# Step 0 of a one-core attention and tile-FFN kernel: x in two halves, first weights split on GpSimd, array warmed by 512-column products

## The chip, the cores and the metric

One core of a Trainium2 chip runs the whole program. The metric is device time in microseconds. Three runs of the kernel before gave 309.85, 310.03 and 310.3; their median is 310.03.

## The reference, cut to what matters

x has shape (2, 2048, 256). Two residual blocks follow one another:

```
h   = gelu(layernorm(x) @ W1{q,k,v} + b1{q,k,v});  q, k, v = h @ W2{q,k,v} + b2{q,k,v}
x  += layernorm(((q @ k.T) / sqrt(256*512) * tril) @ v) * ln_w + ln_b
idx = argmax_t(position_table(2048, 32) @ sign(tile_sigs).T)      # one tile of 8 for each position
x  += layernorm(x) @ W[idx].T + b[idx]
```

The choice of a tile depends on the position table and the signs of the tile signatures alone, not on x.

## The kernel before, in words

The 4096 rows are worked off in 8 steps of 512 rows (4 steps for each batch element). Every product with float32 inputs is made of three fp32r products: each operand is split into a rounded part ("hi") and its rest ("lo"), and hi*hi + hi*lo + lo*hi is accumulated. So every weight needs two operations before its first use: a copy that rounds it into `w_sp[:, i, 0]`, and a subtraction that writes the rest into `w_sp[:, i, 1]`. The weights are numbered 0 to 5: W1q, W1k, W1v, W2q, W2k, W2v. Weight 3 is scaled first, and weight 5 has its row means taken off first (`w_mean`, counted by the semaphore `w_even`).

A step's front part is: layer norm of x into `xn`; 8 transposes into two PSUM banks; rounding and rest of `xnT`; six groups of 6 products of 512 columns for the hidden layer (`front_h`), each followed by gelu and rounding on ScalarE (`hidden`) and the rest on VectorE (`h_rest`); then q, k, v, the transposes of k (`front_ktok`) and the scores. The back part (state and output of linear attention) of step s is interleaved with the front part of step s+1. There is no scheduler: each engine's program is written out by hand in the order in which it runs, and engines wait for each other's semaphores. An engine never goes past an instruction that waits.

Step 0 has extra work. TensorE runs `route_scores` between the first transposes and the first hidden group: 16 products of the position table (`peT`, laid over `hT`) with the signs `sgn_r`, which wait for the table's transfer (`table_in`) and for three small VectorE operations (`route_signs`, semaphore `rv`). GpSimd makes constants (identity, triangles, a blank row), the reciprocal standard deviations (`rstd_lead`, whose central operation is a power), and `residual(0)`, which adds the layer norm's bias row to x. VectorE runs `route_argmax` and `route_ranks` for the choice of tiles. The statistics of step 1's x (`lead_stat(1)`, `lead_var(1)`, `rstd_lead(1)`) are made during step 0 too, and ScalarE normalises x of step 1 (`lead_norm(1, ...)`) in four pieces between `q_rounded`, `k_rounded` and `v_rounded` of step 0.

## Time and profile before

| | |
|---|---|
| median of three runs | 310.03 us |
| span of the profiled execution | 307.9 us (2.1 us less than the median) |
| TensorE busy | 289.4 us, 94% of the span |
| VectorE, ScalarE, GpSimd busy | 75%, 64%, 53% |
| first hidden product of step 0 starts | 12.72 us |
| first transposes of step 1 start | 36.34 us |

A timeline row gives the start in us, the time it covers in us, the engine, the line of the kernel, the operation, the tiles written and read with their shapes, how many instructions were merged, and in brackets how long the engine had been idle and what ended that. Busy shares are averages; in step 0 the engines wait for each other far more than in the later steps.

### The profile page before, as it was taken

The numbers are of one execution on the slowest core, as the hardware profiler recorded it, in microseconds if no ns is written. First come the engines' busy times: TensorE is split into PE (matmuls) and PEld (weight loads), VectorE is DVE, ScalarE is ACT, GpSimd is POOL, SyncE is SP. The second block draws the span as 40 slices with busy tenths as digits, with TensorE's granted clock in tenths as the row PEclk, the third lists the DMA queues.
The fourth block names the chain that finished last, engine by engine and source line by source line (L and its number), as shares of the span: only waits on it lengthen the run. The fifth ranks groups of instructions, "written<-read, shape, count | busy, mean of one in ns | idle before, by whom it ended". The sixth has DMA issues, their size and how long they took to land.

```text
span 307.9 us, 5596 instructions
## 1 busy us (share of the span) xinstructions
PE 289.4 (94%) x1874; PEld 259.1 (84%) x1874; DVE 231.8 (75%) x514; ACT 198.4 (64%) x391; POOL 163.3 (53%) x229
## 2 busy tenths in 40 slices
PE   6899999999999999999999999999999898889990
PEld 6778989898789889888978898889898898889970
DVE  4697779789977966986697579758956888767661
ACT  2388567767586778578667865886877554688000
POOL 3710622190479174927544653557364575777771
PEclk9989999999999999999999999999999999999997
DMA  8819961001110211111131100027021361393220
GB/s 203 285 43 245 362 206 34 0 2 68 34 57 18 90 51 38 42 60 38 36 104 36 56 18 0 2 73 200 2 92 36 88 198 55 126 333 119 80 68 18
DMA packets 24193, 27.84 MB, mean 90 GB/s; under 512 B 4643, under 2 KB 22052, under 8 KB 24102
## 3 DMA queue, kind: packets, MB, share of 16 engines
q1 hardware_dynamic: 15750, 13.29, 14.6%
q0 software_dynamic: 3296, 8.64, 8.1%
q10 hardware_dynamic: 5120, 5.55, 5.6%
q8 instruction: 16, 0.26, 0.4%
q14 instruction: 11, 0.09, 0.1%
HBM read 13.95 MB, written 14.44 MB: 92 GB/s over the span
## 4 chain that ended last, share of the span: by engine, by line
PE 59%; DVE 18%; issue 5%; DMA 5%; ACT 5%; POOL 4%; SPq 1%; POOLq 0%; DVEq 0%; ACTq 0%
PE ring L463 33%; PE o_ps L463 9%; PE s_ps L463 5%; PE sc_ps L463 5%; POOL out_dram L1688 3%; DMA w_stage<-w1v 3%; DVE xres L1179 2%; PE ring L476 2%; PE w_ps L463 1%; PE ring L557 1%; DMA slot_rows<-sorted_rows 1%; DVE xnT L1098 1%; DMA sorted_rows<-xres,slot_i 1%; DVE st L1186 1%; DVE hT L1103 1%
## 5 line engine op out<-in xcount | busy, mean ns | idle before, releaser
L463 PE MATMUL ring<-xnT,w_sp 128*128 128x512 f32 x288 | 75.0, 406 | 2.1 <-issue 1.0
L463 PEld LDWEIGHTS ring<-xnT,w_sp 128*128 128x128 f32 x288 | 53.1, 193 | 14.8 <-DVE hT L1103 1.9
L836 ACT ACTIVATE ring<-ring,b_cols 128x512 f32<-128x512 f32 x48 | 31.7, 660 | 24.5 <-PE ring L463 23.4
L463 PE MATMUL ring<-hT,w_sp 128*128 128x512 f32 x192 | 46.4, 397 | 0.0
L1103 DVE TENSOR_TENSOR hT<-ring,hT 128x512 fp32r<-128x512 f32 x48 | 32.6, 684 | 13.9 <-ACT hT L839 13.3
L463 PEld LDWEIGHTS ring<-hT,w_sp 128*128 128x128 f32 x192 | 35.4, 188 | 8.1 <-DVE hT L1103 0.2
L1643 POOL DMA_INDIRECT sorted_rows<-xres,slot_i x30 | 30.7, 1023 | 8.4 <-issue 6.6
L1609 POOL TENSOR_TENSOR vtok<-v,vtok 128x512 fp32r<-128x512 f32 x14 | 17.7, 1282 | 30.7 <-ACT vtok L858 30.7
L1590 POOL TENSOR_SCALAR nm<-mv 128x4 f32<-128x4 f32 x8 | 1.8, 229 | 57.5 <-DVE mv L1085 57.5
L839 ACT CAST hT<-ring 128x512 fp32r<-128x512 f32 x48 | 28.2, 587 | 1.5
L463 PE MATMUL o_ps<-state,qT 128*128 128x256 f32 x174 | 26.6, 290 | 0.0
L1688 POOL DMA_INDIRECT out_dram<-slot_rows x22 | 21.6, 980 | 6.7 <-issue 6.1
L463 PE MATMUL s_ps<-vtok,ktok 128*128 128x256 f32 x168 | 24.9, 285 | 0.0
L463 PEld LDWEIGHTS o_ps<-state,qT 128*128 128x128 f32 x174 | 23.2, 190 | 1.4 <-issue 0.5
L463 PEld LDWEIGHTS ring<-w_sp,hT 128*128 128x128 f32 x192 | 23.4, 188 | 0.6
L463 PE MATMUL ring<-w_sp,hT 128*128 128x256 f32 x192 | 23.9, 281 | 0.0
L1179 DVE SCALAR_TENSOR_TENSOR xres<-cen,rs,xres 128x256 f32<-128x256 f32 x32 | 22.1, 703 | 0.3 <-issue 0.3
L463 PEld LDWEIGHTS s_ps<-vtok,ktok 128*128 128x128 f32 x168 | 22.1, 191 | 0.0
L463 PE MATMUL sc_ps<-qT,kT 128*128 128x128 f32 (+1 forms) x174 | 21.7, 281 | 0.0
L1109 DVE SCALAR_TENSOR_TENSOR qT<-ring,b_cols,qT 128x512 fp32r<-128x512 f32 x16 | 12.0, 751 | 12.3 <-ACT qT L845 12.3
L463 PEld LDWEIGHTS sc_ps<-qT,kT 128*128 128x128 f32 x174 | 20.4, 192 | 0.2
L1151 DVE TENSOR_TENSOR state<-s_ps,state 128x512 fp32r<-128x512 f32 x27 | 18.3, 677 | 2.4 <-ACT state L878 2.4
(210 smaller groups left out, 614.2 us busy)
## 6 DMA issues: line engine op xcount, KB each, us to landing
sorted_rows<-blank ACTq DMA_DIRECT2D x1, 5032.0 KB, 18.1
xt<-x SPq DMA_DIRECT2D x8, 512.0 KB, 3.5
slot_rows<-sorted_rows SPq DMA_DIRECT2D x22, 136.0 KB, 3.0
w_stage<-tile_w SPq DMA_DIRECT2D x8, 256.0 KB, 2.8
h<-sorted_rows SPq DMA_DIRECT2D x15, 136.0 KB, 3.6
hT<-position_table POOLq DMA_DIRECT2D x1, 512.0 KB, 6.5
sorted_rows<-xres,slot_i POOLq DMA_INDIRECT x30, 2.6
row_stage<-rows ACTq DMA_DIRECT2D x1, 384.0 KB, 7.7
```

The costliest lines, as they stand in the source:

```text
L463: last = te.matmul(o, lhs[k][a], rhs[k][c], start=start and k == 0 and i == 0, stop=stop and k == n - 1 and i == 2, skip_group_check=check)
L476: last = te.transpose(ring[k][:, cols(c)], xn[:, c, cols(k)], ident[:, :])
L557: last = te.transpose(ring[(14 + n) % 3][:, cols(i)], k32[:, i % 2, cols(2 * n + i // 2)], ident[:, :])
L836: nc.scalar.activation(full, ring[(2 + m) % 3][:, :], ACT.Gelu, bias=b1c[:, m // 2, m % 2:m % 2 + 1]).then_inc(gelu, 1)
L839: nc.scalar.copy(hT[:, m, 0, :], full).then_inc(h_hi, 1)
L1103: nc.vector.tensor_tensor(hT[:, m, 1, :], ring[(2 + m) % 3][:, :], hT[:, m, 0, :].bitcast(F32), ALU.subtract).then_inc(h_lo_dve, 1)
L1109: nc.vector.scalar_tensor_tensor(out=qT[:, 1, j, :], in0=ring[(8 + j) % 3][:, :], scalar=b2c[:, Q, j:j + 1], in1=qT[:, 0, j, :].bitcast(F3 ...
L1151: nc.vector.tensor_tensor(state[:, 1, :], s_ps[:, :], state[:, 0, :].bitcast(F32), ALU.subtract).then_inc(s_lo, 1)
L1179: nc.vector.scalar_tensor_tensor(out=xres[s % XR][:, c, 0:C], in0=cen[:, c, :], scalar=rs2[:, c:c + 1], in1=xres[s % XR][:, c, 0:C], op0=A ...
L1609: nc.gpsimd.tensor_tensor(vtok[:, 1, 2 * j:2 * j + 2, :], v32[:, 2 * j:2 * j + 2, :], vtok[:, 0, 2 * j:2 * j + 2, :].bitcast(F32), ALU.sub ...
L1643: pool.indirect_dma_start(out=sorted_rows, out_offset=bass.IndirectOffsetOnAxis(ap=at, axis=0), in_=xres[s % XR][:, c, :], in_offset=None) ...
L1688: pool.indirect_dma_start(out=out_rows, out_offset=bass.IndirectOffsetOnAxis(ap=row_buf(n)[:, PLACE:PLACE + 1].bitcast(I32), axis=0), in_= ...
```

## The change

The change touches step 0 only. Half of x (two of four chunks) is loaded, normalised and transposed ahead of the other half. ScalarE rounds only weight 0 and VectorE makes only its rest; GpSimd does both for weights 1 to 5. GpSimd issues the position table's transfer after its constants and after the first half of x is there, where it was its first instruction. The rows `rows3` are loaded by the sync queue behind the weights, where ScalarE's queue loaded them, and x of step 1 comes last. `residual(0)` and `rstd_lead(1)` stand behind the five splits on GpSimd. On TensorE, 34 transposes of the identity are replaced by 8 products of 512 columns ahead of the first transposes and 4 more between the two halves of them.

```diff
-WARM = 34
+WARM = (8, 4)
@@ sync
-            load_x(0)
+            sp.dma_start(xt[0][:, 0:2, :], x_gbp[0, 0][:, 0:2]).then_inc(x_half, 16)
+            sp.dma_start(xt[0][:, 2:CH, :], x_gbp[0, 0][:, 2:CH]).then_inc(x_in[0], 16)
             for i, w in enumerate((w1[Q], w1[K], w1[V], w2[Q], w2[K], w2[V])):
                 sp.dma_start(w_stage[:, i, :, :], w.rearrange("(k p) n -> p k n", p=P)).then_inc(w_in[i], 16)
-                if i == 2:
-                    load_x(1)
+            sp.dma_start(row_stage[:, :, :], rows3.partition_broadcast(P)).then_inc(rows_in_place, 16)
+            load_x(1)
@@ tensor
+            def kept_busy(n):
+                for i in range(n):
+                    te.matmul(ring[2][:, :], warm_r[:, 0:P], warm_r[:, :], start=True, stop=True)
+
+            def first_transposes():
+                te.wait_ge(xn_half, 1)
+                for k in range(KC):
+                    for c in range(2):
+                        te.transpose(ring[k][:, cols(c)], xn[:, c, cols(k)], ident[:, :])
+                kept_busy(WARM[1])
+                te.wait_ge(xn_done, 1)
+                for k in range(KC):
+                    for c in range(2, CH):
+                        last = te.transpose(ring[k][:, cols(c)], xn[:, c, cols(k)], ident[:, :])
+                    last.then_inc(fill, 1)
...
+            te.wait_ge(warm_set, 1)
+            kept_busy(WARM[0])
             te.wait_ge(consts, 2)
-            for i in range(WARM):
-                te.transpose(ring[2][:, 0:P], ident[:, :], ident[:, :])
-            front_transposes(0, True)
+            first_transposes()
             route_scores()
@@ scalar
-            for i in range(5):
-                weights_rounded(i)
-                if i == 2:
-                    xnT_rounded(0)
-            act.wait_ge(small_in, 32)
+            act.wait_ge(w_in[0], 16)
+            nc.scalar.copy(w_sp[:, 0, 0, :, :], w_stage[:, 0, :, :]).then_inc(w1q_hi, 1)
+            xnT_rounded(0)
+            act.wait_ge(cols_in, 16)
             act.wait_ge(rp, 1)
             for m in range(6):
                 hidden(0, m)
-                if m == 2:
-                    weights_rounded(5)
@@ vector
+            nc.vector.memset(warm_r[:, :].bitcast(F32), 1.0).then_inc(warm_set, 1)
             state_cleared()
-            lead_stat(0)
-            lead_var(0)
+            first_half(0)
+            first_half(1)
+            first_norm(0)
+            first_norm(1)
+            dve.wait_ge(w1q_hi, 1)
+            nc.vector.tensor_tensor(w_sp[:, 0, 1, :, :], w_stage[:, 0, :, :], w_sp[:, 0, 0, :, :].bitcast(F32),
+                                    ALU.subtract).then_inc(w1q_lo, 1)
             route_signs()
-            weights_rest((0,))
-            lead_norm()
-
             xnT_rest(0)
-            weights_rest((1, 2))
@@ gpsimd
-            pool.dma_start(peT, pe).then_inc(table_in, 16)
             nc.gpsimd.memset(ident[:, :], 0.0).then_inc(consts, 1)
...
-            rstd_lead(0)
...
-            residual(0)
             nc.gpsimd.memset(blank[:, :], 0.0).then_inc(blank_set, 1)
             pool.wait_ge(blank_set, 1)
             nc.gpsimd.memset(blank[:, PLACE:PLACE + 1].bitcast(I32), NOWHERE).then_inc(blank_set, 1)
+
+            pool.wait_ge(x_half, 16)
+            pool.dma_start(peT, pe).then_inc(table_in, 16)
+            for h in range(2):
+                these = slice(2 * h, 2 * h + 2)
+                pool.wait_ge(var_first, h + 1)
+                nc.gpsimd.tensor_tensor(rs1[:, these], ve1[:, these], half[:, these], ALU.pow).then_inc(rstd_first, 1)
+
+            for i in range(1, 6):
+                pool.wait_ge(w_in[i], 16)
+                if i == 3:
+                    pool.wait_ge(w_scaled, 1)
+                elif i == 5:
+                    pool.wait_ge(w_even, 3)
+                nc.gpsimd.tensor_copy(w_sp[:, i, 0, :, :], w_stage[:, i, :, :]).then_inc(w_hi, 1)
+                pool.wait_ge(w_hi, i)
+                nc.gpsimd.tensor_tensor(w_sp[:, i, 1, :, :], w_stage[:, i, :, :], w_sp[:, i, 0, :, :].bitcast(F32),
+                                        ALU.subtract).then_inc(w_lo, 1)
+
+            pool.wait_ge(rows_in_place, 16)
+            residual(0)
             rstd_lead(1)
             v_rest(0)
```

Two new VectorE functions make one half each: `first_half(h)` runs two bn_stats, two bn_aggr and the addition of EPS, and `first_norm(h)` the two normalisations behind GpSimd's power. VectorE's `w_mean` work for weight 5 is spread between `h_rest(0, 0)`, `h_rest(0, 1)` and `h_rest(0, 2)`; `lead_stat(1)` stands behind `h_rest(0, 3)` and `lead_var(1)` behind `h_rest(0, 4)`.

On GpSimd, at the start of the program, the order before was this (`rs`, `nm`, `sh`, `ve` are the small tiles of `rstd_lead`; `hT<-position_table` is the table's transfer):

```order
L1573 DMA hT<-position_table 64x2048
L1574 MEMSET ident 128x128
...
L1593 TENSOR_TENSOR rs<-ve,half 128x4 [waits var1]
L1595 TENSOR_TENSOR sh<-nm,rs 128x4 [waits rstd1]
L1648 AFFINE_SELECT tril<-tril 128x128
...
L1602 TENSOR_TENSOR xres<-xt,row_stage 128x4x256
L1665 MEMSET blank 128x272
L1667 MEMSET blank 128x1 [waits blank_set]
L1590 TENSOR_SCALAR nm<-mv 128x4 [waits aggr1]
```

In the changed program the same place, from the last constants on, reads:

```order
L1686 MEMSET blank 128x272
L1688 MEMSET blank 128x1 [waits blank_set]
L1691 DMA hT<-position_table 64x2048 [waits x_half]
L1695 TENSOR_TENSOR rs<-ve,half 128x2 [waits var_first] x2
L1703 CAST w_sp<-w_stage 128x512 [waits w_in1]
L1705 TENSOR_TENSOR w_sp<-w_stage,w_sp 128x512 [waits w_hi]
...
L1703 CAST w_sp<-w_stage 128x512 [waits w_even,w_in5]
L1705 TENSOR_TENSOR w_sp<-w_stage,w_sp 128x512 [waits w_hi]
L1626 IOTA xres 128x4 [waits x_half,x_in0,rows_in_place]
L1627 TENSOR_TENSOR xres<-xt,row_stage 128x4x256
L1613 TENSOR_SCALAR nm<-mv 128x4 [waits aggr1]
```

The table's transfer moved from the first place to behind all constants, and ten split operations moved in ahead of `residual(0)` and of step 1's reciprocal deviations.

On VectorE, the changed program from the second half's normalisation to the mean of weight 5 reads (`w_sp<-w_stage,w_sp` is the rest of weight 0, `sgn` the signs for the routing):

```order
L1107 TENSOR_SCALAR xn<-xt,mv,rs 128x256 [waits rstd_first]
L1107 TENSOR_SCALAR xn<-xt,mv,rs 128x256
L1357 TENSOR_TENSOR w_sp<-w_stage,w_sp 128x512 [waits w1q_hi]
L1257 TENSOR_SCALAR sgn<-sig_in 64x8 [waits sigs_in]
L1258 TENSOR_SCALAR sgn<-sig_in 64x8 [waits rv]
L1259 TENSOR_TENSOR sgn_r<-sgn 64x8 [waits rv]
...
L1133 TENSOR_TENSOR hT<-ring,hT 128x512 [waits h_hi]
L1370 TENSOR_SCALAR w_mean<-w_mean 128x2 [waits w_even]
L1372 TENSOR_TENSOR w_stage<-w_stage,w_mean 128x512 [waits w_even]
L1133 TENSOR_TENSOR hT<-ring,hT 128x512 [waits h_hi]
```

The signs came ahead of the normalisation and now come behind it; weight 5's mean is taken off behind the second `h_rest`, where it was taken off ahead of the first.

## Rows read from the trace of the kernel before

**Rows 1.** The page, parts 1 and 2: busy time, and granted clock in tenths.

```profile
PE 289.4 (94%) x1874; PEld 259.1 (84%) x1874; DVE 231.8 (75%) x514; ACT 198.4 (64%) x391; POOL 163.3 (53%) x229
PEclk9989999999999999999999999999999999999997
```

**Rows 2.** Chain that ended last, 0 to 60 us: start, us, engine, tile, line.

```profile
30.92 0.39 DVE kT L1115
...
33.88 0.51 ACT vtok L858
```

**Rows 3.** Timeline of PE, 0 to 45 us.

```profile
9.82 1.09 PE L476 MATMUL ring<-ident,xn 128*128 128x128 f32 x8 [0.88 <-DVE xn L1091]
10.84 1.95 PE L608 MATMUL sc_ps<-sgn_r,hT 64*128 64x8 f32 x16
12.72 6.00 PE L463 MATMUL ring<-xnT,w_sp 128*128 128x512 f32 x18
...
36.34 1.06 PE L476 MATMUL ring<-ident,xn 128*128 128x128 f32 x8 [0.17 <-DVE ktok L1122]
```

**Rows 4.** Window 14 to 18 us: busy by engine, granted clock, DMA.

```profile
14.00:18.00 4.00, 4.00 (x12) 3.14 (x11) 3.19 (x7) 3.18 (x6) 0.00 (x0) 0.57 0.38 131
```

**Rows 5.** Timeline of POOL, 0 to 45 us.

```profile
1.33 0.72 POOL L1573 DMA_DIRECT2D hT<-position_table  x1 [0.83 <-POOLq L1763]
2.05 0.23 POOL L1574 MEMSET ident<- 128x128 f32 x1
...
3.06 0.20 POOL L1583 MEMSET tril<- 128x128 f32 x1
...
8.58 0.37 POOL L1648 TENSOR_SCALAR_AFFINE_SELECT tril<-tril 128x128 f32<-128x128 f32 x1
...
10.62 0.14 POOL L1662 IOTA row_no<- 128x1 f32 x1
...
10.81 2.35 POOL L1602 TENSOR_TENSOR xres<-xt,row_stage 128x1024 f32<-128x1024 f32 x1
13.11 0.32 POOL L1665 MEMSET blank<- 128x272 f32 x1
...
21.40 0.23 POOL L1590 TENSOR_SCALAR nm<-mv 128x4 f32<-128x4 f32 x1 [7.82 <-DVE mv L1085]
...
23.00 0.30 POOL L1595 TENSOR_TENSOR sh<-nm,rs 128x4 f32<-128x4 f32 x1
```

**Rows 6.** DMA issues by line: KB each, us to landing.

```profile
xt<-x SPq DMA_DIRECT2D x8, 512.0 KB, 3.5
...
hT<-position_table POOLq DMA_DIRECT2D x1, 512.0 KB, 6.5
```

**Rows 7.** Groups by line and shape, POOL: busy, mean ns.

```profile
L1609 POOL TENSOR_TENSOR vtok<-v,vtok 128x512 fp32r<-128x512 f32 x14 | 17.7, 1282 | 30.7 <-ACT vtok L858 30.7
...
L1677 POOL TENSOR_SCALAR w_stage<-w_stage 128x255 f32<-128x255 f32 x16 | 15.4, 966 | 0.0
...
L1623 POOL TENSOR_TENSOR rs<-ve,half 128x2 f32<-128x2 f32 x2 | 1.4, 708 | 0.2
```

**Rows 8.** Timeline of ACT, 0 to 45 us.

```profile
25.70 0.59 ACT L895 ACTIVATE xn<-xt,sh,rs 128x256 f32<-128x256 f32 x1
```

**Rows 9.** The page, part 5: the hidden layer's groups on ACT and DVE.

```profile
L836 ACT ACTIVATE ring<-ring,b_cols 128x512 f32<-128x512 f32 x48 | 31.7, 660 | 24.5 <-PE ring L463 23.4
...
L1103 DVE TENSOR_TENSOR hT<-ring,hT 128x512 fp32r<-128x512 f32 x48 | 32.6, 684 | 13.9 <-ACT hT L839 13.3
...
L839 ACT CAST hT<-ring 128x512 fp32r<-128x512 f32 x48 | 28.2, 587 | 1.5
```

**Rows 10.** Timeline of DVE, 0 to 45 us.

```profile
4.36 1.40 DVE L1077 BATCH_NORM_STATS2 st<-xt 128x6 f32<-128x256 f32 x4 [2.89 <-DMA xt<-x]
...
8.39 1.38 DVE L1091 TENSOR_SCALAR xn<-xt,mv,rs 128x256 f32<-128x256 f32 x4 [0.94 <-POOL rs L1593]
```

**Rows 11.** Line L1323 alone: duration ns min/median/max.

```profile
L1323 DVE TENSOR_TENSOR w_sp<-w_stage,w_sp x6: 679/686/1184, 6.8 to 22.6; 128x512 fp32r<-128x512 f32 x6
```

More of the change, by code:

```diff
@@ L100, in mk_seq_kernel @@
         ident = sb("ident", [P, P])
+        warm_r = sb("warm_r", [P, GT], F32R)
         tril = sb("tril", [P, P])
@@ L153, in mk_seq_kernel @@
         w_in = [sem(f"w_in{i}") for i in range(6)]
-        small_in = sem("small_in")
+        x_half = sem("x_half")
+        cols_in = sem("cols_in")
+        rows_in_place = sem("rows_in_place")
         sigs_in = sem("sigs_in")
@@ L166, in mk_seq_kernel @@
         w_lo = sem("w_lo")
+        w1q_hi = sem("w1q_hi")
+        w1q_lo = sem("w1q_lo")
+        warm_set = sem("warm_set")
         stat1 = sem("stat1")
         aggr1 = sem("aggr1")
+        aggr_first = sem("aggr_first")
+        var_first = sem("var_first")
+        rstd_first = sem("rstd_first")
+        xn_half = sem("xn_half")
         var1 = sem("var1")
@@ L499, in front_h @@
                         bank_free(s, m - 3)
-                    if first and m % 2 == 0:
-                        te.wait_ge(w_lo, m // 2 + 1)
+                    if first and m == 0:
+                        te.wait_ge(w1q_lo, 1)
+                    elif first and m % 2 == 0:
+                        te.wait_ge(w_lo, m // 2)
                     for k in range(KC):
@@ L515, in front_qk @@
                 if first:
-                    te.wait_ge(w_lo, 4 + which)
+                    te.wait_ge(w_lo, 3 + which)
                 for j in (2 * which, 2 * which + 1):
@@ L821, in _ @@
             act.dma_start(sig_in[:, :], sigs2).then_inc(sigs_in, 16)
-            act.dma_start(b_cols[:, :, :].rearrange("p a k -> p (a k)"), bias_cols).then_inc(small_in, 16)
-            act.dma_start(row_stage[:, :, :], rows3.partition_broadcast(P)).then_inc(small_in, 16)
+            act.dma_start(b_cols[:, :, :].rearrange("p a k -> p (a k)"), bias_cols).then_inc(cols_in, 16)
             act.wait_ge(consts, 3)
@@ L1073, in _, with first_half, first_norm @@
         def _(dve):
+            def first_half(h):
+                dve.wait_ge(x_in[0] if h else x_half, 16)
+                for c in (2 * h, 2 * h + 1):
+                    nc.vector.bn_stats(st1[:, c, :], xt[0][:, c, :]).then_inc(stat1, 1)
+                dve.wait_ge(stat1, 2 * h + 2)
+                alone(dve, gate_dve)
+                for c in (2 * h, 2 * h + 1):
+                    last = nc.vector.bn_aggr(mv1[:, c, :], st1[:, c, :])
+                last.then_inc(aggr_first, 1)
+                dve.wait_ge(aggr_first, h + 1)
+                these = slice(2 * h, 2 * h + 2)
+                nc.vector.tensor_scalar(ve1[:, these], mv1[:, these, 1], EPS, None, ALU.add).then_inc(var_first, 1)
+            def first_norm(h):
+                dve.wait_ge(rstd_first, h + 1)
+                for c in (2 * h, 2 * h + 1):
+                    last = nc.vector.tensor_scalar(xn[:, c, :], xt[0][:, c, :], mv1[:, c, 0:1], rs1[:, c:c + 1],
+                                                   ALU.subtract, ALU.mult)
+                last.then_inc(xn_done if h else xn_half, 1)
             def lead_stat(s):
@@ L1081, in lead_var @@
                 alone(dve, gate_dve)
-                if s:
-                    dve.wait_ge(shift1, s)
+                if s > 1:
+                    dve.wait_ge(shift1, s - 1)
                 for c in range(CH):
@@ L1086, in lead_var @@
                 last.then_inc(aggr1, 1)
-            def lead_norm():
-                dve.wait_ge(rstd1, 1)
-                for c in range(CH):
-                    last = nc.vector.tensor_scalar(xn[:, c, :], xt[0][:, c, :], mv1[:, c, 0:1], rs1[:, c:c + 1],
-                                                   ALU.subtract, ALU.mult)
-                last.then_inc(xn_done, 1)
             def xnT_rest(s):
@@ L1338, in _ @@
                                     ALU.mult).then_inc(w_scaled, 1)
-            weights_rest((3, 4))
+            h_rest(0, 0)
             dve.wait_ge(w_in[5], 16)
             nc.vector.tensor_reduce(w_mean[:, :], w_stage[:, 5, :, :], AX_X, ALU.add).then_inc(w_even, 1)
+            h_rest(0, 1)
             dve.wait_ge(w_even, 1)
@@ L1348, in _ @@
                                     w_mean[:, :].unsqueeze(2).broadcast_to([P, KC, C]), ALU.add).then_inc(w_even, 1)
-            dve.wait_ge(small_in, 32)
+            h_rest(0, 2)
+            dve.wait_ge(cols_in, 16)
             nc.vector.tensor_scalar(b2c[:, Q, :], b2c[:, Q, :], INV_SCALE, None, ALU.mult).then_inc(w_scaled, 1)
-            h_rest(0, 0)
-            h_rest(0, 1)
+            h_rest(0, 3)
             lead_stat(1)
+            h_rest(0, 4)
             lead_var(1)
-            h_rest(0, 2)
-            h_rest(0, 3)
-            weights_rest((5,))
-            h_rest(0, 4)
             h_rest(0, 5)
@@ L1361, in _ @@
             q_rest(0, (0,))
+            dve.wait_ge(w_lo, 3)
+            dve.wait_ge(rows_in_place, 16)
             route_argmax()
@@ L1667, in _ @@
             nc.gpsimd.memset(blank[:, PLACE:PLACE + 1].bitcast(I32), NOWHERE).then_inc(blank_set, 1)
+            pool.wait_ge(x_half, 16)
+            pool.dma_start(peT, pe).then_inc(table_in, 16)
+            for h in range(2):
+                these = slice(2 * h, 2 * h + 2)
+                pool.wait_ge(var_first, h + 1)
[12 more added lines that the diff above has]
+            residual(0)
             rstd_lead(1)
```

36 lines of the change are left out of this document (11 added, 25 removed).

## The prediction, made before the changed kernel was run

> **What bounds the kernel now.** I read the page first. TensorE is busy 94% of the span and holds its full clock in nearly every slice [rows 1]. So a microsecond gained or lost ahead of the steady part arrives at the end one for one, provided it shifts the first transposes of step 1, which start at 36.34 [rows 3]. That instant, T, is what I forecast.
>
> Then I read the timeline of TensorE for the first 37 us. The first hidden product stands at 12.72, straight behind the 16 routing products, which end then [rows 3]: with no idle time in between, TensorE itself, by its routing products, sets this start. The 18 products from 12.72 take 6.00 us [rows 3]. The granted clock falls to half there: the mean over 14 to 18 us is 0.57 [rows 4], which is 0.43 x 4 / 0.5 = 3.4 us at half clock (1.2 instead of 2.4 GHz), so 1.7 us of work lost. Ahead of the fall the array had had 0.88 us of idle, 8 transposes and 16 routing products of 8 columns [rows 3]. Without it a hidden product costs (6.00 - 1.7) / 18 = 0.24 us.
>
> From 25.7 to 36.3 the chain no longer lies on TensorE. It runs through the second rest of k (30.92), v, ScalarE's roundings of v (33.88) and the rest of ktok, which ends TensorE's wait ahead of T [rows 2, 3]. All of that stands behind ScalarE's queue, in which the first piece of step 1's normalisation starts at 25.70 [rows 8]. This normalisation needs GpSimd's `rstd_lead(1)`, which before was done at 23.3 [rows 5], with 2.4 us to spare.
>
> **The change part by part.**
>
> *Start of the hidden products.* x in halves, and five ScalarE and five VectorE operations fewer, bring `xn` and `xnT` forward. VectorE, with 1.40 us for four statistics and 1.38 for four normalisations [rows 10], has the second half done at about 8.2 (behind GpSimd's second power, below) instead of 8.39 + 1.38 = 9.77. But TensorE goes through the routing products first, and they wait for the table. Its transfer was GpSimd's first instruction and took 6.5 us from issue to landing [rows 6]. Now it stands behind the constants: 2.05 to 3.26 is 1.21 us, 8.58 to 10.76 is 2.18, and the blank row 0.32 plus 0.15 for its wait and last memset is 0.47 [rows 5]. Begun at about 1.0 (the first transfer's slot falls free), they end at 4.9. The first half of x is there by then, since the whole of it was used at 4.36 before [rows 10]. The table then lands at 4.9 + 6.5 = 11.4. The routing products occupy 10.84 to 12.72, 1.88 us [rows 3], so the hidden products start at 13.3, 0.6 us later than before. Bounds for the transfer: I don't expect it quicker than an x load of the same 512 KB, 3.5 us [rows 6], and 0.7 more for GpSimd's issue [rows 5], which gives 9.1; it is slower if it shares the engines with the later weights, by some 1 us. I take the transfer's own row, and 11.4, since both times other loads are under way.
>
> *The clock.* The 8 products come early (from about 1.5) and end by 5; the second lot of 4 stands between the transposes, at about 8 to 9.7. From then to the table's landing the array idles or runs narrow work, as it did before the fall in [rows 3, 4]. So I leave the 1.7 us of half clock where it was. The 34 transposes taken out were under no one's wait. If four products run at half clock, they cost 4 x 512 / 1.2 GHz = 1.7 us ahead of the last four transposes, and the table at 11.4 still hides that; without that cover they would cost 1 us.
>
> *The weights of the hidden layer.* GpSimd starts to split at about 7.4 (issue 0.72 [rows 5], then two powers at 0.71 [rows 7] and their waits). A split is a copy and a subtraction. The subtraction has the shape and types of `vtok<-v,vtok`, 1.28 us [rows 7]. The copy has no row. Below, it can't take less than the blank memset of 272 columns, 0.32 us [rows 5], brought to 512 columns, 0.6. Above, the tensor_scalar with 255 columns at 0.966 us [rows 7], brought to 512 columns, 1.9. A plain copy is nearer to the memset: I take 0.8, a split of 2.2 us with its wait. Splits of weights 1 to 4 end at 16.2, and the hidden and q products that want them start at 13.3 + 12 x 0.24 + 1.7 = 17.9 and later (weight 1 is split at 9.6). So these splits are hidden, up to the copy's upper end too (four of 3.3 us end at 20.6, weight 4 is wanted at 25).
>
> The page "GPSIMD Engine Reference", section 3.1, of the Trainium skill gives 1.03 cycles for an element of a one-input body; by that the copy would take about 0.6 us and the sum below would be 0.2 us smaller. No row here shows such a copy.
>
> *Weight 5 and what stands behind it.* This is the part that costs. GpSimd waits for `w_even` = 3, which VectorE gives only behind `h_rest(0, 1)`. From the start of the hidden products: 12 products at 0.24 with the half clock, 2.9 + 1.7 = 4.6; gelu and rounding 0.66 + 0.59 with waits 1.4; the rest 0.68 [rows 9]; subtracting the mean, of the same size, with its scaling and waits 1.0. Sum 7.7: 13.3 + 7.7 = 21.0. Then on GpSimd: split 2.2, to 23.2; `residual(0)` 2.35 plus 0.15 for its iota and wait [rows 5], to 25.7; `rstd_lead(1)` from 21.40 to 23.30, 1.9 [rows 5], to 27.6. The other input, `lead_var(1)`, is ready before 25.7: behind 24 products (5.7 + 1.7), 1.4 for ScalarE, 0.7 for `h_rest(0, 3)`, 1.4 of statistics, 0.7 for `h_rest(0, 4)` and 0.5 it is 13.3 + 12.1 = 25.4.
>
> *What then waits.* ScalarE's first normalisation of step 1 can't start before 27.6; before, it ran at 25.70 [rows 8]. Queued behind it are q's second rounding, the second piece, and k's four operations. Back to back these end with k's first rounding 3.1 us behind 27.6, VectorE takes the first rest and the three small operations on the bias row, 1.56 us, and starts the second rest of k at 27.6 + 4.66 = 32.3 instead of 30.92 [rows 2]: 1.4 us later. Everything from there to T was tight (v, its roundings and ktok follow one another in the chain [rows 2]), so T moves to 37.7.
>
> *Rest.* `residual(0)` comes 12 us later, so x of step 2 is loaded at about 25.7 beside the blank rows; it is wanted near 45, and the tile weights at 36, so I count nothing; without that cover it would be the time by which a load of some 5 us is late. Moving `rows3` behind the weights costs nothing: its first user is VectorE at 26. Sum: 310.03 + 1.4 = **311.4 us** (the profiled execution: 307.9 + 1.4 = 309.3).
>
> **The rivals.**
>
> *Faster: the table isn't late, and the clock holds.* If the transfer lands by about 10, the routing starts when the signs and transposes are done, the hidden products at about 12.0, and with the 12 wide products just ahead the array may escape the half clock. Then `w_even` = 3 comes at 12.0 + 6.0 = 18.0, `rstd_lead(1)` ends at 24.6, the second rest of k starts at 29.3, 1.6 us earlier: 308.4. It decides from 26.3 on: that is the end of `rstd_lead(1)` at which T stays. For it: wide products are real work, and the transfer's own minimum is lower than 6.5 us. Against: the same narrow routing work stands ahead of the hidden products as before. Chance 0.23.
>
> *The change does little.* Table early but half clock kept, or late with the clock kept: `rstd_lead(1)` at 26.3, plus or minus 0.6, so 309.5 to 310.6. Chance 0.2.
>
> *Signs late, by the port.* VectorE's one rest of a weight that met GpSimd's long addition took 1184 ns where the median is 686 [rows 11]: it started at 12.53, inside 10.81 to 13.16 [rows 5]. Now the rest of weight 0 and the signs (from about 8.2) fall among GpSimd's splits, of 0.8 and 1.28 us in turn. If each of the four waits out one of them, the signs are ready at 12.7, the hidden products start at 14.6, and the time is 312.8. Against: the signs are tiny and two have one input. Chance 0.12.
>
> The page "SBUF — State Buffer", section "SBUF: two separate sides", of the Trainium skill says that VectorE and GpSimd share a port pair under an exclusive lock, taken by VectorE operations with two SBUF inputs or in a two-port mode. By that rule the 1184 ns agree.
>
> The forecast itself, table about 11.4 and weight 5's split ahead of `rstd_lead(1)`, has 0.45.
>
> **How the numbers follow.** A measurement of this kernel tells 0.2%, 0.6 us. Slower by more than that: 0.45 + 0.12 = 0.57; within: 0.2; faster: 0.23. Low end: the faster rival at 308.4. High end: the copy at 1.9 instead of 0.8 adds 1.1 to the forecast, 312.5, and the port rival gives 312.8; both with a table 0.3 later, 313.1. Range 308.4 to 313.1; that of the likeliest case alone is 310.7 to 312.5.
>
> **What would show it.** Right: TensorE idle ahead of its routing products, ended by the table's transfer, near 11.4; the first hidden product near 13.3; a fall of the granted clock in the hidden products; GpSimd idle ahead of the last copy until `w_mean`; ScalarE idle ahead of `xn<-xt,sh,rs` until GpSimd's `sh`, near 27.6; T near 37.7. Wrong: a table that lands before 10, hidden products all at 0.24 us, no wait of ScalarE for `sh`, or a wait for weights 1 to 4 on TensorE (GpSimd's copy far above 1.9 us, or transfers late).

## The result, and the profile after

The changed kernel takes 315.42 us (median of 4 runs, 314.28 to 315.79). The kernel before took 309.94 beside it (309.77 to 310.3). The ratio is 1.0165, with a 95% interval of 1.0148 to 1.0182: 5.5 us slower, where 1.4 had been forecast. The ratios of this document leave out executions more than 1.5% above the fastest of the same kernel (2 of 12 in f2, 3 in f3, 3 in g1, 2 in g3), so that a ratio can differ a little from that of the medians, which count all. The profiled execution of after took 314.28, the lowest of the four. Its span is 312.4 us against 307.9, so 4.5 us of the loss stand in the trace.

TensorE is busy a little more than before, in a longer span, and stays the bound (the page, part 1, of after).

```profile
PE 290.8 (93%) x1852; PEld 259.0 (83%) x1852; DVE 232.2 (74%) x512; ACT 195.5 (63%) x386; POOL 172.3 (55%) x237
```

The next rows are the timeline of PE of after (start, time covered, engine, line, operation, tiles, count, idle time before it and what ended that). They answer to [rows 3].

```profile
7.12 1.08 PE L489 MATMUL ring<-ident,xn 128*128 128x128 f32 x4 [1.82 <-DVE xn L1107]
7.85 2.06 PE L483 MATMUL ring<-warm_r 128*128 128x512 f32 x4
9.71 1.05 PE L494 MATMUL ring<-ident,xn 128*128 128x128 f32 x4
13.57 3.54 PE L636 MATMUL sc_ps<-sgn_r,hT 64*128 64x8 f32 x16 [2.81 <-DMA hT<-position_table]
17.04 10.00 PE L474 MATMUL ring<-xnT,w_sp 128*128 128x512 f32 x36
...
40.59 1.06 PE L502 MATMUL ring<-ident,xn 128*128 128x128 f32 x8 [0.27 <-DVE ktok L1152]
```

T, the first transposes of step 1, is 40.59 instead of 36.34: 4.25 of the 4.5 us are lost ahead of it. The first hidden product moved from 12.72 to 17.04, which is 4.3 us by itself. Two rows make it. The array stands idle for 2.81 us until the table's transfer ends, and the 16 routing products then take 3.54 us, where they took 1.95 [rows 3]. Behind them the 36 hidden products take 9.84 us (17.04 to 26.88), 0.9 us less than before (12.72 to 23.45), and from there to T it is 13.71 us instead of 12.89, 0.8 us more: 4.3 - 0.9 + 0.8 is the 4.25 by which T moved.

The chain that ended last of after, 0 to 50 us (start, us, piece), runs through the same places:

```profile
4.29 9.14 DMA hT<-position_table
...
13.57 3.54 PE sc_ps L636 x16
17.11 4.32 PE ring L474 x12
...
23.57 0.70 DVE w_stage L1372
24.40 0.61 POOL w_sp L1703
25.09 1.29 POOL w_sp L1705
26.47 2.38 POOL xres L1627
...
30.44 0.21 POOL sh L1618
30.68 0.60 ACT xn L922
...
35.18 0.16 DVE kT L1145
```

Twelve hidden products at full clock would be 2.9 us; 4.32 says that part of them ran at half clock (1.2 instead of 2.4 GHz) too. Behind them stand weight 5's mean (L1372), its split, the residual and step 1's reciprocal deviations. ScalarE waits for the last of these, as the timeline of ACT of after shows:

```profile
30.68 0.60 ACT L922 ACTIVATE xn<-xt,sh,rs 128x256 f32<-128x256 f32 x1 [1.45 <-POOL sh L1618]
```

The timeline of POOL of after, against [rows 5] and [rows 7]:

```profile
4.02 0.10 POOL L1688 MEMSET blank<- 128x1 int32 x1
4.29 0.74 POOL L1691 DMA_DIRECT2D hT<-position_table  x1 [0.16 <-issue]
...
7.16 0.61 POOL L1703 CAST w_sp<-w_stage 128x512 fp32r<-128x512 f32 x1
7.85 1.28 POOL L1705 TENSOR_TENSOR w_sp<-w_stage,w_sp 128x512 fp32r<-128x512 f32 x1
...
26.43 2.42 POOL L1627 TENSOR_TENSOR xres<-xt,row_stage 128x1024 f32<-128x1024 f32 x1
```

The constants end at 4.12, not 4.9, so the transfer was issued 0.6 us earlier than forecast; the copy takes 0.61 us, not 0.8. The transfer is what was mis-sized. These are the parts 3 of the page for two stretches of after, from its issue to 8.2 us and from there to its landing (packets, MB, share of the 16 engines):

```profile
q1 hardware_dynamic: 1262, 1.21, 99.6%
q0 software_dynamic: 1, 0.01, 0.8%
...
q1 hardware_dynamic: 501, 0.73, 66.7%
q0 software_dynamic: 79, 0.52, 42.5%
```

And the same of the kernel before, from 4.2 us, before which q0 has no packet, to its landing:

```profile
q0 software_dynamic: 80, 0.52, 63.9%
q1 hardware_dynamic: 267, 0.26, 28.5%
q10 hardware_dynamic: 206, 0.20, 21.4%
```

q0 is the queue on which GpSimd's transfers go, the table's 80 packets here. Before, they began 2.9 us after the issue, behind 672 packets of SP's queue (q1, 1.3 to 4.2 us), and moved in 3.6 us, beside 473 packets of the weights and of q10, half of the engines' time. After, they began 3.9 us after it, behind 1262 packets that kept the engines full, and took 5.3 us beside 501, two thirds of the engines' time. That is 9.1 instead of 6.5. That the packets ahead and beside make the difference fits these rows; no run isolates it.

VectorE's timeline of after shows its operations beside GpSimd's splits, which run from 7.16 to 11.41:

```profile
6.24 0.73 DVE L1107 TENSOR_SCALAR xn<-xt,mv,rs 128x256 f32<-128x256 f32 x2
7.23 2.04 DVE L1107 TENSOR_SCALAR xn<-xt,mv,rs 128x256 f32<-128x256 f32 x2 [0.27 <-POOL rs L1695]
9.20 1.09 DVE L1357 TENSOR_TENSOR w_sp<-w_stage,w_sp 128x512 fp32r<-128x512 f32 x1
10.21 1.22 DVE L1257 TENSOR_SCALAR sgn<-sig_in 64x8 f32<-64x8 f32 x1
11.47 0.16 DVE L1258 TENSOR_SCALAR sgn<-sig_in 64x8 f32<-64x8 f32 x1
```

The same two normalisations take 0.73 us alone and 2.04 beside the first split. A row of 8 elements takes 1.22 and ends with the split, and the next two, behind it, take 0.16 each. The signs are ready at 11.83, and the table hides it.

### The profile page after: what moved, and what is told of

Same layout as the page of the kernel before. It is cut to its first block, busy times and chain, and to the rows that moved or that the text cites. A ratio compares the mean times of both kernels' runs of the same rounds, so it can differ in the third digit from the quotient of the medians.

```text
span 312.4 us, 5556 instructions
## 1 busy us (share of the span) xinstructions
PE 290.8 (93%) x1852; PEld 259.0 (83%) x1852; DVE 232.2 (74%) x512; ACT 195.5 (63%) x386; POOL 172.3 (55%) x237
## 3 DMA queue, kind: packets, MB, share of 16 engines
q0 software_dynamic: 3296, 8.64, 8.0%
## 4 chain that ended last, share of the span: by engine, by line
PE 61%; DVE 15%; POOL 7%; ACT 6%; DMA 5%; issue 4%; POOLq 0%; SPq 0%; DVEq 0%; ACTq 0%
PE ring L474 33%; PE o_ps L474 9%; PE s_ps L474 5%; PE sc_ps L474 5%; POOL out_dram L1730 3%; DMA hT<-position_table 3%; PE w_ps L474 2%; PE ring L502 2%; DVE xres L1209 2%; PE ring L585 1%; DMA slot_rows<-sorted_rows 1%; PE sc_ps L636 1%; DVE st L1216 1%; DVE hT L1133 1%; PE w_ps L628 1%
## 5 line engine op out<-in xcount | busy, mean ns | idle before, releaser
L474 PEld LDWEIGHTS s_ps<-vtok,ktok 128*128 128x128 f32 x168 | 22.1, 191 | 0.0
L1730 POOL DMA_INDIRECT out_dram<-h x15 | 15.7, 1044 | 8.2 <-issue 4.1
```

The lines of the kernel that those rows point to most:

```text
L474: last = te.matmul(o, lhs[k][a], rhs[k][c], start=start and k == 0 and i == 0, stop=stop and k == n - 1 and i == 2, skip_group_check=check)
L1730: pool.indirect_dma_start(out=out_rows, out_offset=bass.IndirectOffsetOnAxis(ap=row_buf(n)[:, PLACE:PLACE + 1].bitcast(I32), axis=0), in_= ...
```

## The experiments

Each kernel was timed beside the kernel before on its chip, and the ratio is what counts. On the three chips of the experiments the kernel before takes 322.5 to 323.4 us, not 309.9. The changed kernel, repeated there (f1 below), has T at 41.01, near its 40.59, but a span of 323.9 instead of 312.4. So some 11 us lie behind T, and nearly all of them behind the transposes of step 7, the last step (217.75 in f1, 217.20 in after): from there to the end f1 takes 106.2 us and after 95.2. Its row of granted clocks on the page is lower in the last slices than [rows 1], which is a part of it (40 slices of 8 us):

```profile
PEclk9569999999999999999999999999999999998698
```

All kernels of the experiments show it, and why it is so stays open. The kernel before was not traced there; g4 below, which measured the same as it (1.0012), has T at 36.62, so 36.34 serves as a measure within some 0.3 us.

**First round: one part each.** e1, from the changed kernel, issues the table's transfer first again:

```diff
+            pool.dma_start(peT, pe).then_inc(table_in, 16)
             nc.gpsimd.memset(ident[:, :], 0.0).then_inc(consts, 1)
...
-            pool.wait_ge(x_half, 16)
-            pool.dma_start(peT, pe).then_inc(table_in, 16)
```

> The changed kernel with the position table's transfer back as GpSimd's first instruction. Theory A (the late table holds up the routing products, and with them all hidden products): the table lands near 8, the routing products start when the signs are ready near 11.8, the first hidden product moves from 17.04 to between 13.8 and 15.4, and the time falls by 1.6 to 3.3 us, to 312.1 to 313.8. Rival B (GpSimd's chain of splits, residual and reciprocal deviations sets the first transposes of step 1 whatever the table does): under 0.5 us less than the changed kernel's 315.4.

Measured: 326.87 against 322.71, ratio 1.0116 [1.0074, 1.0158]. The table landed at 9.6, and yet little came back: Theory A wanted 1.6 to 3.3 us, and the interval overlaps that of the changed kernel on the experiments' chips (f1, 1.0121 to 1.0178), so that no gain is shown. PE's timeline of e1:

```profile
13.20 2.96 PE L636 MATMUL sc_ps<-sgn_r,hT 64*128 64x8 f32 x16 [2.54 <-DVE sgn_r L1259]
```

and DVE's:

```profile
10.62 0.69 DVE L1357 TENSOR_TENSOR w_sp<-w_stage,w_sp 128x512 fp32r<-128x512 f32 x1 [2.71 <-ACT w_sp L933]
11.23 0.57 DVE L1257 TENSOR_SCALAR sgn<-sig_in 64x8 f32<-64x8 f32 x1
...
12.03 1.11 DVE L1259 TENSOR_TENSOR sgn_r<-sgn 64x8 fp32r<-64x8 f32 x1
```

A second wait stood behind the first. With the table issued early, weight 0 landed 8.2 us after its issue instead of 4.3 (6.7 and 6.0 in f2 and g1, whose table is early too, but 4.0 in the kernel before), and its rest is ahead of the signs in VectorE's order; then the signs, beside GpSimd's split from 10.76 on, took 0.57 and 1.11 us instead of 0.16. They were ready at 13.1. The array, after 2.5 us of idle time, fell to half clock again: the granted clock is 0.97 from 12 to 14 us and 0.50 from 14 to 20.

e2, from the changed kernel, warms with the old 34 transposes and without the 4 wide products:

```diff
-                kept_busy(WARM[1])
...
-            te.wait_ge(warm_set, 1)
-            kept_busy(WARM[0])
             te.wait_ge(consts, 2)
+            for i in range(34):
+                te.transpose(ring[2][:, 0:P], ident[:, :], ident[:, :])
```

> The changed kernel with the 34 transposes of the identity in place of the 8 and 4 wide products. Theory A: the wide products end too early and leave the array idle, so the clock is at half through the routing products (3.5 us instead of 1.95) and into the hidden ones; with the transposes, which run until about 7, the clock may be up for the routing products: 0.5 to 2 us less than 315.4. Rival B: the array idles for 4 us behind the transposes of xn either way, the clock is down either way, and the time stays within 0.5 us of 315.4.

Measured: 327.15, ratio 1.0141 [1.0117, 1.0165]. PE's timeline has the same picture, as Rival B said, so the wide products neither make the loss nor prevent it:

```profile
13.42 3.54 PE L635 MATMUL sc_ps<-sgn_r,hT 64*128 64x8 f32 x16 [3.60 <-DMA hT<-position_table]
```

e3 makes only the table late in the kernel before:

```diff
-            pool.dma_start(peT, pe).then_inc(table_in, 16)
             nc.gpsimd.memset(ident[:, :], 0.0).then_inc(consts, 1)
...
+            pool.wait_ge(x_in[0], 16)
+            pool.dma_start(peT, pe).then_inc(table_in, 16)
             exact = dict(allow_small_or_imprecise_dtypes=True)
```

> The kernel before with one edit: the table's transfer is issued near 4.4 us, behind the first x, instead of at 1.33. Theory A: it lands near 13.4, the first hidden product starts at 15.4 to 17, and the time is 312.7 to 314.3, most of what the whole change costs. Rival B (the rest of the change is what costs): the transfer lands by 11 as its 6.5 us say, and the time is 310.0 to 310.8.

Measured: 329.06, ratio 1.0204 [1.0178, 1.0230]: this one edit costs 2.0%, no less than the whole change and more than Theory A's 2.7 to 4.3 us. Issued at 5.04, the table landed at 17.0, 3.6 us later than in after. So e3 shows that a late table alone can cost this much, but not how much of the change's own loss it makes. The page of e3 gives the transfer (KB, us to landing), longer still than in after:

```profile
hT<-position_table POOLq DMA_DIRECT2D x1, 512.0 KB, 12.0
```

and PE's timeline the wait and the half clock behind it:

```profile
17.22 3.54 PE L608 MATMUL sc_ps<-sgn_r,hT 64*128 64x8 f32 x16 [6.24 <-DMA hT<-position_table]
```

e4 gives the kernel before only GpSimd's splits of weights 1 to 5, with `residual(0)` and `rstd_lead(1)` behind them:

```diff
-            for i in range(5):
-                weights_rounded(i)
-                if i == 2:
-                    xnT_rounded(0)
+            act.wait_ge(w_in[0], 16)
+            nc.scalar.copy(w_sp[:, 0, 0, :, :], w_stage[:, 0, :, :]).then_inc(w1q_hi, 1)
+            xnT_rounded(0)
...
+            for i in range(1, 6):
...
+                nc.gpsimd.tensor_copy(w_sp[:, i, 0, :, :], w_stage[:, i, :, :]).then_inc(w_hi, 1)
...
+            residual(0)
             rstd_lead(1)
```

> The kernel before with one edit: GpSimd splits weights 1 to 5, with residual(0) behind them, nothing else moved. Theory A (the splits themselves are cheap, 1.95 us each, and ready in time when the mean of weight 5 is taken off early): GpSimd ends rstd_lead(1) near 25.5, ScalarE isn't held up, and the time is 309.3 to 310.4. Rival B (GpSimd is too slow for five splits): ScalarE waits for sh by 1 us and more, 311 or more.

Measured: 321.57 (12 runs), ratio 0.9976 [0.9960, 0.9992]: a small gain, and the only one of the study. The profiled execution is the fastest of the twelve (320.40), and g2 below, which keeps the splits, doesn't repeat the gain. ScalarE waited 0.59 us for `sh`, against the expectation. PE's timeline of e4 has the first 18 hidden products without half clock, then a new wait:

```profile
12.70 4.47 PE L465 MATMUL ring<-xnT,w_sp 128*128 128x512 f32 x18
18.12 4.68 PE L465 MATMUL ring<-xnT,w_sp 128*128 128x512 f32 x18 [0.95 <-DVE hT L1104]
```

VectorE comes late with the rests because its small operations take longer beside the splits, as one row of its timeline shows (on `b_cols`, 0.25 us in the trace of after at 24.78):

```profile
16.23 1.25 DVE L1351 TENSOR_SCALAR b_cols<-b_cols 128x2 f32<-128x2 f32 x1
```

**Second round: the changed kernel again, and three repairs of it.** f1 is the changed kernel, unedited, for the chip's own ratio.

> The changed kernel itself, unaltered, as the measure for the three that follow on the same chip. Expected: 1.4 to 1.8% slower than the kernel before, the table's transfer landing near 13.4, the routing products near 3.5 us long.

Measured: 326.85 against 322.49, ratio 1.0150 [1.0121, 1.0178]; the table took 8.7 us, the routing products 3.54 from 13.10. The window 14 to 18 us of f1 (busy and count of PE, PEld, DVE, ACT, POOL, then granted clock, DMA) shows half clock outright:

```profile
14.00:18.00 4.00, 4.00 (x16) 3.71 (x16) 0.00 (x0) 0.00 (x0) 3.33 (x4) 0.50 0.03 10
```

f2 has e1's edit, and the signs ahead of the normalisation:

```diff
             first_half(1)
+            route_signs()
             first_norm(0)
...
-            route_signs()
             xnT_rest(0)
```

> The changed kernel with the table's transfer as GpSimd's first instruction, and the signs made ahead of first_norm. With the table alone moved, the signs came at 13.2, behind weight 0's rest, and took the table's place as what is waited for. Theory A (two things hold up the routing products, table and signs, one behind the other): they now start behind the transposes of xn, at 10.5 to 11, the first hidden product at 12.7 to 14.4, and the time is 2 to 4 us less than the changed kernel's. Rival B (weights that land later, since the table goes ahead of them, set the start: weight 0 lands near 10, its rest is ready near 11.5): less than 1.5 us.

Measured: 322.75 (12 runs), ratio 0.9990 [0.9960, 1.0021], as Theory A said. No loss is left that the interval would show. PE's timeline of f2 has no idle time ahead of the routing, which runs at full clock, and T is 36.55. Among the 36 hidden products the clock still falls (0.57 from 14 to 18 us):

```profile
11.04 1.95 PE L636 MATMUL sc_ps<-sgn_r,hT 64*128 64x8 f32 x16
12.91 10.23 PE L474 MATMUL ring<-xnT,w_sp 128*128 128x512 f32 x36
```

f3 leaves the late table and puts 7 wide products into the gap:

```diff
             first_transposes()
+            kept_busy(7)
             route_scores()
```

> The changed kernel with 7 more wide products between the transposes of xn and the routing products, where the array idled for 2.8 us. Theory A (the idle array runs the routing products at half clock, 3.5 us instead of 1.95): routing products of 1.95 to 2.6 us, and 1 to 2 us less than the changed kernel. Rival B (the routing products are slow whatever stands ahead of them, or the half clock is only put off to the hidden products): within 0.6 us of the changed kernel.

Measured: 323.88 (12 runs), ratio 1.0024 [0.9990, 1.0059]. PE's timeline of f3: the table is no earlier than 12.4, but the routing products and the 36 hidden ones behind them run at full clock (0.24 each). T is 36.59, 4.4 us earlier than in f1: 0.6 because the table landed that much earlier in this execution (8.1 us instead of 8.7), 1.6 by the routing products, and 2.2 by the hidden ones (8.53 us to the end of the 36, where f1 takes 10.74). Theory A counted only the routing products. The rows:

```profile
10.22 1.86 PE L483 MATMUL ring<-warm_r 128*128 128x512 f32 x7
12.50 1.92 PE L636 MATMUL sc_ps<-sgn_r,hT 64*128 64x8 f32 x16 [0.42 <-DMA hT<-position_table]
14.35 8.69 PE L474 MATMUL ring<-xnT,w_sp 128*128 128x512 f32 x36
```

f4 leaves both and takes weight 5 off the chain. Its mean and step 1's statistics come ahead of `h_rest(0, 0)`, and `rstd_lead(1)` ahead of the residual:

```diff
-            h_rest(0, 0)
+            lead_stat(1)
...
-            h_rest(0, 1)
+            lead_var(1)
...
+            h_rest(0, 0)
+            h_rest(0, 1)
             h_rest(0, 2)
...
+            rstd_lead(1)
             pool.wait_ge(rows_in_place, 16)
             residual(0)
-            rstd_lead(1)
```

> The changed kernel with lead_stat(1), the mean of weight 5 and lead_var(1) ahead of h_rest(0, 0), where VectorE idled for 7.9 us, and with rstd_lead(1) ahead of residual(0) on GpSimd. Theory A (the chain that was forecast, weight 5, residual, reciprocal deviations, costs by itself what ScalarE waits for sh, and part of that was hidden by TensorE): ScalarE's wait of 1.45 us ahead of xn is gone, the first transposes of step 1 come 0.7 to 1.1 us earlier, and so does the end. Rival B (that chain is hidden entirely by the late hidden products): no change beyond 0.3 us.

Measured: 325.58, ratio 1.0097 [1.0068, 1.0126], 1.3 us less than f1 by the medians, with intervals that overlap by little. ACT's timeline of f4 has no wait for `sh`, which POOL had ready at 22.1:

```profile
27.64 0.59 ACT L922 ACTIVATE xn<-xt,sh,rs 128x256 f32<-128x256 f32 x1
```

In its profiled execution the routing products took 2.04 us behind a wait of 1.99 us for the table, so that its T (38.29) owes 1.5 us to the clock. What the freed chain gives is read behind the hidden products: from the end of the 36 to T it is 12.97 us here and 13.70 in f1, 0.7 us less, the low end of what was expected.

**Third round: can it be beaten?** g1 is f2 and f4 together, with the scaling of `b_cols` moved up to the signs.

> The changed kernel with all repairs: table first, signs (and the scaling of the q bias) ahead of first_norm, lead_stat(1), the mean of weight 5 and lead_var(1) ahead of h_rest(0, 0), rstd_lead(1) ahead of residual(0). Theory A (these waits add up): 1 to 1.5 us less than with table and signs first alone, which measured the same as the kernel before: ratio to the kernel before 0.994 to 0.998, first transposes of step 1 near 35.3. Rival B (freeing the chain only moves VectorE operations into GpSimd's splits, which they then wait out): ratio 0.998 to 1.002.

Measured: 324.76 against 323.44 (12 and 35 runs), ratio 1.0020 [0.9983, 1.0058]: no better than f2, and outside what Theory A expected. From the end of the 36 hidden products to T it is 12.89 us, as in the kernel before, so the chain is free here too. But with no idle time ahead of them the routing products took as long as at half clock, and T is 38.68:

```profile
11.40 3.57 PE L636 MATMUL sc_ps<-sgn_r,hT 64*128 64x8 f32 x16
```

g2 is e4 with the mean of weight 5 behind one `h_rest`, `b_cols` ahead, `lead_var(1)` one `h_rest` later, and `rstd_lead(1)` ahead of the residual.

> The kernel before with GpSimd's splits (0.9976 of the kernel before), and now also the first h_rest between the mean's operations, the q bias scaled ahead of them, and rstd_lead(1) ahead of residual(0). Theory A: TensorE's wait of 0.95 us ahead of the fourth hidden group and ScalarE's of 0.59 go, first transposes near 34.6, ratio 0.993 to 0.997. Rival B: VectorE's small operations wait out GpSimd's splits wherever they stand, ratio stays at 0.9976.

Measured: 323.99, ratio 1.0030 [0.9998, 1.0062]. The idle time of e4 fell from 0.95 to 0.32 + 0.23 us, and T is 35.32, 0.2 us earlier than e4's (34.6 was expected). The time didn't follow, and in this trace 2.0 us were lost in step 1. GpSimd's `residual(1)` came 4 us later than in e4, behind a wait of 4.94 us for the tile's bias, and stood beside an operation of VectorE of 32 elements, which takes 0.21 us in e4 and before (rows of POOL and DVE of g2):

```profile
44.35 2.39 POOL L1603 TENSOR_TENSOR xres<-xt,row_stage 128x1024 f32<-128x1024 f32 x1
44.35 2.43 DVE L1252 TENSOR_TENSOR held<-w_stage 128x32 f32<-128x32 f32 x1
```

The transposes of step 2 start 30.82 us behind T, in e4 28.81.

g3 is g1 with 3 wide products ahead of the routing (`kept_busy(3)`).

> The kernel with all repairs and 3 wide products between the transposes of xn and the routing products. Theory A (wide products just ahead of the narrow ones keep the clock up into the hidden products): they delay the hidden products by 0.3 to 0.7 us but save the 1.7 us of the half-clock stretch in some executions: 0.3 to 1 us less than without. Rival B: the clock falls anyway, 0.3 to 0.7 us more than without.

Measured: 325.84, ratio 1.0059 [1.0022, 1.0095]. That is 0.4% above g1, with intervals that overlap, so the three products gave nothing. In its profiled execution x came late (TensorE waits 6.96 us ahead of its first transposes, in the other changed kernels 1.8 to 2.5), so no row of it is read.

g4 is the kernel before with 14 wide products in place of the 34 transposes.

```diff
-            for i in range(WARM):
-                te.transpose(ring[2][:, 0:P], ident[:, :], ident[:, :])
+            te.wait_ge(warm_set, 1)
+            for i in range(14):
+                te.matmul(ring[2][:, :], warm_r[:, 0:P], warm_r[:, :], start=True, stop=True)
```

> The kernel before with 14 products of 512 columns in place of the 34 transposes, nothing else. Theory A (what is run to warm the array doesn't matter while the narrow routing products stand behind it): ratio 0.998 to 1.002, clock down for some 3.4 us in the hidden products as before. Rival B (the wide products hold the clock): 1 to 1.7 us less, ratio 0.995 to 0.997.

Measured: 324.12, ratio 1.0012 [0.9977, 1.0048], with a first lot of 18 hidden products of 5.99 us from 12.92 and a granted clock of 0.57 from 14 to 18, as in [rows 3, 4]. Wide products in the place of transposes change nothing that can be measured here.

**All traces side by side.** One execution of each kernel, in us: idle time of TensorE ahead of the routing products, the time these take, from the first of the 36 hidden products to the end of the last, from there to T, T, and the start of the transposes of step 7.

| | idle ahead | routing | 36 hidden | from there to T | T | step 7 |
|---|---|---|---|---|---|---|
| before | 0 | 1.95 | 10.73 | 12.89 | 36.34 | 212.73 |
| after | 2.81 | 3.54 | 9.84 | 13.71 | 40.59 | 217.20 |
| f1, after again | 2.65 | 3.54 | 10.74 | 13.70 | 41.01 | 217.75 |
| e1, table first | 2.54 | 2.96 | 10.61 | 13.72 | 40.42 | 217.16 |
| e2, old warming | 3.60 | 3.54 | 10.93 | 13.71 | 41.53 | 218.05 |
| e3, before, table late | 6.24 | 3.54 | 10.79 | 12.89 | 44.37 | 220.92 |
| e4, before, splits | 0 | 1.95 | 9.94 | 12.88 | 35.52 | 211.87 |
| f2, table and signs first | 0 | 1.95 | 10.07 | 13.57 | 36.55 | 213.28 |
| f3, gap filled | 0.42 | 1.92 | 8.53 | 13.71 | 36.59 | 213.33 |
| f4, chain freed | 1.99 | 2.04 | 10.68 | 12.97 | 38.29 | 214.65 |
| g1, all repairs | 0 | 3.57 | 10.89 | 12.89 | 38.68 | 215.06 |
| g2, e4 reordered | 0 | 1.94 | 9.60 | 12.88 | 35.32 | 213.92 |
| g4, before, wide | 0 | 1.95 | 10.80 | 12.90 | 36.62 | 213.00 |

Three things can be read off. From the hidden products' end to T it is 13.57 to 13.72 us wherever weight 5's split and the residual stand ahead of `rstd_lead(1)` in the changed kernel, and 12.88 to 12.97 everywhere else: that chain costs 0.6 to 0.8 us. The routing products took 2.96 to 3.54 us in the five traces with 2.5 us and more of idle time ahead of them, and 1.92 to 2.04 in the others, g1 excepted, which had none and took 3.57. And behind the transposes of step 7 the kernels of the experiments take from 106.2 to 109.6 us, in no order that their edits in step 0 would explain. So one total can carry 3 us that have nothing to do with step 0, and T and step 7 tell more of an edit than a single time.

## Why the prediction was right and wrong

The direction was right, and so was the path that was forecast; the size was off by 4.0 us, outside the range. Of these, 2.9 are in T (40.59 instead of 37.7), 0.2 behind it in the trace, and 0.9 lie between trace and median (after's median is 3.0 us above its span, before's 2.1). By its steps:

*Start of the hidden products* is the term that failed. Forecast: table at 11.4, hidden products at 13.3. Measured: 13.43 and 17.04. Of the 3.7 us between, 2.0 are the transfer and 1.7 the routing products. The transfer was given its old 6.5 us "since both times other loads are under way", and took 9.1 (8.7 in f1, 12.0 in e3). The load is not alike in the two places: before, 672 packets of SP's queue went ahead of it, now 1262. The price named for that in the prediction, "some 1 us", was too low by 1.6, and it wasn't taken into the sum; the earlier issue (4.29 instead of 4.9) gave 0.6 back. That the table alone can carry the loss is shown by e3 (2.0%); that an early table and early signs remove it, by f2 (0.999).

*The clock* is the second part of the same failure. I left the 1.7 us of half clock where it was. In after, the routing products take 3.54 instead of 1.95, 1.6 us more, and the 36 hidden ones 9.84 (17.04 to 26.88) where 36 x 0.24 is 8.64, 1.2 us more: 2.8 in all, of which 1.6 stand ahead of the first hidden product, where none had been put. The prediction saw the idle time ahead of the routing but gave it no price beyond that of before, where it was 0.88 us ahead of the transposes. How much the clock is worth, f3 shows: with the gap filled and the table still late the kernel is at 1.0024, and of the 4.4 us between its T and f1's the clock makes 3.8. What decides the clock in one execution is not settled: f4's routing, behind 1.99 us of idle time, was at full clock, and g1's, behind none, was not.

*The weights of the hidden layer.* Right: splits 1 to 4 ended at 17.5 (16.2 forecast), and TensorE waited for none. GpSimd waited 2.21 us for the scaling of weight 3, which the sum left out and which cost nothing. The copy took 0.61, not 0.8. The prediction's estimate from the Trainium skill ("GPSIMD Engine Reference", section 3.1), 0.6 us, agrees with the row; the page's 1.03 cycles for an element alone give an estimate of 512 x 1.03 / 1.2 GHz = 0.44 us, to which a fixed part has to be added.

*Weight 5 and what stands behind it.* Right in itself. From the first hidden product to the mean took 7.2 us (17.04 to 24.26; forecast 7.7), from there to `sh` 6.4 (to 30.64; forecast 6.6). The end, 30.64 instead of 27.6, carries the 3.7 us from above less the 0.7 by which these two terms were too long; that they offset a part of the miss is luck.

*What then waits.* Right: ScalarE waited 1.45 us for `sh`, and from its normalisation to the second rest of k it was 4.5 us (30.68 to 35.18; forecast 4.7). What this chain costs by itself is 0.7 us ahead of T in the traces (f4 against f1) and 1.3 us by their medians, which the clock moves too; that this is near the 1.4 forecast for the whole is chance, since the forecast had the chain and the later start together.

*Rest.* Right: from T to the end it is 271.8 us in after and 271.6 before.

*The rivals.* What the port rival expected did happen, though it wasn't the cause in after: the second half's normalisation was done at 9.27, not at 8.2, and the stretched signs at 11.83, behind the table's cover. With the cover gone (e1) they cost most of what the early table should have given, together with the late weight 0, which the prediction hadn't foreseen. The Trainium skill's page "SBUF — State Buffer", section "SBUF: two separate sides", reserves the lock to VectorE operations with two SBUF inputs or in a two-port mode. The measured one-input normalisations waited too (2.04 against 0.73). One-input rows are quicker than two-input ones in after (the scaling of 128x512 in L1363 takes 0.42 us, a subtraction of that size 0.69), which would fit such a mode; that they ran in it no run shows. The faster rival needed the table by 10. f2 had it, at 8.0 by issue plus transfer (1.33 + 6.7), and ended level, not 1.6 us faster: the half clock stayed, 1.4 us of it among the hidden products, and ScalarE still waited 1.31 us for `sh`.

*Where the change's own gain went.* With both waits removed (f2), half the x, ten splits on GpSimd and the wide products are worth 0.1% with an interval that holds zero. The splits alone gave 0.24% in e4, with an interval that ends at 0.9992; T and step 7 agree in size (0.8 and 0.9 us earlier than before). In g2 their gain is at T and is lost again in step 1.

What stays open: why the transfer on GpSimd's queue starts 3 to 4 us after its issue and takes 6.0 to 12.0 us; why weight 0 lands late behind an early table in the changed kernel and not before; what chooses the clock in one execution. Early signs with a late table were not run; by the trace of after they would have nothing to give, being ready 1.6 us ahead of the table as it is. The 1.1 us by which the median of after lies beyond its profiled execution (315.42 - 314.28) are not explained by one trace.

## What to carry to other kernels

A transfer's duration is no fixed property of it: the same 512 KB took 6.0 to 12.0 us here. When its issue is moved behind other loads, count the packets of every queue that are then ahead of it and beside it, and bound the landing from above by all of them. An idle gap in front of TensorE's narrow products can cost twice, once as the gap and again as half clock behind it: it did so in each of the five traces with a gap of 2.5 us and more, and filling it with wide products gave the loss back with the table still late (f3). That there is no gap doesn't secure the clock (g1). Before taking one wait away, ask which is second: the early table alone gave no gain that is clear of noise, because the signs were ready only at 13.1. And an operation that is moved in time changes what it stands beside: g2 lost in step 1 what it had won in step 0.

## What was unexpected of the hardware

- The table's transfer of 512 KB on GpSimd's queue took 6.0 (g1), 6.5 (before), 6.7 (e4, f2, g2, g4) and 8.3 us (e1) when issued at 1.33, 8.1 to 9.1 us (f3, f4, f1, e2, after) when issued at 4.3, and 12.0 us (e3) when issued at 5.04.
- The 16 routing products of 8 columns took 1.95 us at full clock and 3.54 at half clock (f1, granted clock 0.50).
- In after, the row of granted clocks reads 9 in all slices but the last, though the routing products took 3.54 us and twelve products 4.32. From 18 to 20 us after and f1 both run 6 products of 512 columns, where f3 runs 10; the clock reads 1.00 in after and 0.50 in f1. The same holds for g1. Where the rows contradict each other, the durations are to be believed.
- Beside a split on GpSimd, VectorE's operations of a few elements took 0.49 to 1.25 us instead of 0.16 to 0.25 (after, e1, e4). Beside the residual's 2.4 us one took 2.43 (g2, above) and one 2.12 (f4):

```profile
22.47 2.12 DVE L1378 TENSOR_SCALAR b_cols<-b_cols 128x2 f32<-128x2 f32 x1
```
